# Second attention step with channels in the rows and eight transposes back to nodes, and a shorter reciprocal square root, in a four-layer graph network

## The chip, the core and the metric

The kernel runs on one core of one Trainium2 chip. The metric is the device time of one execution in microseconds; a kernel's number is the median of its runs. The engines are TensorE (PE; its weight loads are PEld), VectorE (DVE), ScalarE (ACT), GpSimd (POOL, which here issues the gathers) and SyncE (SP, which issues the other transfers). Each works through its own list of instructions in order, and they meet at semaphores.

## The reference

There are 8 graphs of 1024 nodes with 128 channels in float32, each with a 1024x1024 adjacency matrix of about 1.6% ones. Four layers follow each other, and each ends in `x = layernorm(x + layer(x))` without gain or bias:

```python
x = _layernorm(x + L0(adj, x))   # max over the first 25 neighbours of each node, then a projection and relu
x = _layernorm(x + L1(x, adj))   # graph attention with leaky relu scores, elu
x = _layernorm(x + L2(x, adj))   # the same with other weights
x = _layernorm(x + L3(x, adj))   # the layer that the change touches
```

The last layer is dot-product attention over the whole graph, applied twice:

```python
mask = where(adj == 1, 0.0, -1000.0)
score = (x @ att_W) @ x.T / sqrt(128)
att = softmax(score + mask, axis=-1)          # 1024 x 1024, the same in both steps
for W, b in ((W0, b0), (W1, b1)):
    y = tanh(att @ (y @ W + b))               # y starts as x
```

`_layernorm(x)` is `(x - mean) / sqrt(var + 1e-5)` over the 128 channels of a node.

## The kernel before

A graph's nodes are held as `xs[slot]`, eight tiles of 128 nodes in the partitions by 128 channels, for two graphs in turn (`slot`). Graphs 0 to 5 run in a hardware loop of three turns with two graphs each, graphs 6 and 7 are written out behind it. For each engine there is one function `graph(b, slot, in_loop)`, and its body is the order of that engine's work; nothing is planned by a program. Each also carries work for the graphs ahead, put by hand into places where the engine would wait:

- The neighbours' maximum of layer 0 for graph b+1 is made during graph b. POOL gathers 21 of the 25 neighbour rows of each tile of 128 nodes by indirect transfers, one instruction for each neighbour and tile (L483), 168 in a graph. The rows go into `gathered`, a ring of three tiles (`RING`). DVE reduces a tile with a maximum (`pool_tile`, L1132 and L1133), and `rows_pooled` frees the ring's place. So the gather of tile t waits for the pooling of tile t-3 (L476, L479), and for every pair of tiles also for the list of row numbers that DVE computes (`find_keys`, `find_members`, L1099, signal `rows_ready`). The table `SIDE` (L82) says in which place of DVE's order each of these pieces stands: tile 5 of graph b+1 stands at "last step", tile 6 at "half" and tile 7 at "end", all around the second attention step. POOL is one graph further ahead there: its gather of tile 0 of graph b+2 waits for the pooling of tile 6 of graph b+1.
- The other 4 neighbours of each node come from products with one-hot matrices: `make_hot` on ACT or DVE, `pick` on PE (16 matmuls of 512 columns each, L760) and `max_pick` on DVE (L1189), eight of them in a graph.
- `feed` converts and packs the adjacency of the graphs ahead (ACT L502, a transposing DMA, PE L707), and `count_first` with `take_count` counts neighbours (PE L735 to L740, ACT L526).

In the last layer PE makes the logits of a tile of 128 nodes (L942, L945), DVE its row maximum (L1315), ACT the exponential (L633); PE multiplies with a diagonal of reciprocals and so transposes it (L958), and ACT puts it into `probs_t` (L640), which holds the attention with source nodes in the partitions. The first step's product (`first_step`, L929) has the channels in the rows of its result: `values` (nodes by channels) is the stationary operand, 512 columns of `probs_t` the moving one. ACT takes tanh of each half of 512 nodes into `xt`, channels by nodes (L645), PE projects from it (L786), ACT copies the result to `values` (L571), and then comes the second step (L973 to L978):

```python
for t in range(T):
    for m in range(T):
        last = nc.tensor.matmul(low_t[:, t, :], probs_t[:, m, t * P:(t + 1) * P], values[:, m, 0:C], ...)
    if t % HALF == HALF - 1:
        att_heads.raised_by(last)
```

Here each matmul has a 128x128 block of the attention as stationary operand and 128 columns of `values` moving, so that the result has nodes in the rows. ACT takes tanh of each half (L655) into `head`, which is another view of `xt`'s memory, and DVE adds it to `xs` (L1334), makes the statistics of that half (`half_stats`, L1194), pools tile 6 between the two halves, and normalises (`layer_norm`, L1196). PE goes on with `feed`, `pick` 7 and the counting for graph b+2. In PE's trace a float32 matmul and its weight load stand as two records each, a transpose as one.

`layer_norm` is called four times in a graph. It aggregates the statistics, then computes the reciprocal square root for the 8 tiles on DVE with operations on 128x8 elements: add epsilon (L1203), shift right (L1204), subtract from a constant (L1206), three rounds of Newton's iteration of three operations each (L1209, L1210, L1212), and the offset for ACT (L1214). `link` puts a drain of DVE behind each. Then DVE scales the first four tiles (L1218) and ACT the other four (L563).

## Time and profile before

| | |
|---|---|
| median of 3 runs | 2911.93 us (2911.41 to 2938.62) |
| profiled execution, device time | 2927.49 us |
| its span in the trace | 2925.5 us |
| mean granted TensorE clock | 0.77 of full speed |
| PE busy | 1708.1 us (58% of the span) |
| PE weight loads | 1227.0 us (42%) |
| DVE busy | 1381.1 us (47%) |
| ACT busy | 923.4 us (32%) |
| POOL busy | 1258.4 us (43%), of it 1254.7 us in 1280 gather instructions (L483) |
| second attention step (L975) | 1024 matmul records, 118.7 us |
| first attention step (L929) | 256 matmul records, 131.3 us |
| tanh behind the second step (L655) | 16, 9.4 us |
| add behind it (L1334) | 16, 11.0 us |

The first three lines are times, the others come from the page of the profiled execution. No engine is busy for more than 58% of the span, so the busy times alone don't say what bounds the kernel. The profiled execution's time is 15.6 us above the median of the runs. A row of a timeline gives the start in us from the span's start, the busy time in us, the engine, the line of the kernel, the operation, its output and inputs, and how many instructions are merged in it; in brackets stands the idle time of the engine ahead of it and what ended it ("issue": nothing that the profile shows; "remote": a semaphore whose sender the profile can't name).

### The profile page before, as it was taken

The page shows a single profiled execution, that of the slowest core. Times are in us where ns is not written, and L with a number is a line of the kernel's source. Part 1 is how long each engine was busy: PE and PEld are TensorE (multiplying, and loading weights), DVE is VectorE, ACT ScalarE, POOL GpSimd, SP SyncE. Part 2 cuts the span into 40 slices and gives each one's busy share as a digit, 9 for nine tenths or more (in the row PEclk, how much of TensorE's full clock was granted, in tenths as well). Part 3 has the DMA queues.
Part 4 walks back from the last instruction along what each step waited for, and adds up shares of the span by engine and source line. Part 5 has one row for each costly group of instructions (what it writes and reads, how often), then busy time and mean ns, then how long its engine had stood idle before and what let it go on. Part 6 is the DMA issues. An engine that isn't in the chain of part 4 may idle for free.

```text
span 2925.5 us, 27567 instructions
## 1 busy us (share of the span) xinstructions
PE 1708.1 (58%) x8804; PEld 1227.0 (42%) x8804; DVE 1381.1 (47%) x3485; ACT 923.4 (32%) x1283; POOL 1258.4 (43%) x1307
## 2 busy tenths in 40 slices
PE   1655666536675367664475645646565555656778
PEld 0533553325443245342453434424353334534655
DVE  3654564336643347433464434544534445442642
ACT  1000433324333234333232343223422324223223
POOL 5366324553344553444444443544425544255000
PEclk9977677768787668876687866877778777787789
DMA  4221212222122221222222220222312222021001
GB/s 126 60 68 43 71 38 91 56 58 67 46 91 54 73 60 56 78 68 52 57 73 70 69 74 26 87 63 68 74 34 74 66 67 73 17 67 52 22 15 37
DMA packets 145466, 178.53 MB, mean 61 GB/s; under 512 B 91165, under 2 KB 108458, under 8 KB 145322
## 3 DMA queue, kind: packets, MB, share of 16 engines
q1 hardware_dynamic: 104362, 92.76, 11.5%
q0 software_dynamic: 40960, 83.97, 10.7%
q8 instruction: 76, 1.25, 0.2%
q14 instruction: 68, 0.56, 0.1%
HBM read 155.66 MB, written 4.19 MB: 55 GB/s over the span
## 4 chain that ended last, share of the span: by engine, by line
PE 36%; another core or an unknown queue 26%; issue 16%; DVE 11%; ACT 5%; DVEq 4%; DMA 1%; SPq 0%; ACTq 0%
PE big L860 5%; PE side L958 4%; PE spare L760 4%; PE big L929 3%; PE big L975 3%; PE big L786 3%; DVEq L68 3%; PE big L942 2%; PE big L807 1%; DVE pooled L1132 1%; PE big L760 1%; PE big L797 1%; PE big L851 1%; DVE stats L1194 1%
## 5 line engine op out<-in xcount | busy, mean ns | idle before, releaser
L483 POOL DMA_INDIRECT gathered<-in_x_dram,rows x1280 | 1254.7, 980 | 1445.0 <-DVE pooled L1133 648.4
L860 PE MATMUL big<-values,probs_t 128*128 128x129 f32 x1792 | 265.4, 303 | 147.6 <-issue 146.6
L760 PE MATMUL spare<-hot,x_part 128*128 128x512 f32 x1088 | 294.7, 420 | 52.1 <-issue 30.9
L860 PEld LDWEIGHTS big<-values,probs_t 128*128 128x128 f32 x1792 | 247.6, 216 | 166.2 <-issue 161.4
L760 PEld LDWEIGHTS spare<-hot,x_part 128*128 128x128 f32 x1088 | 213.1, 200 | 111.0 <-issue 64.6
L1132 DVE TENSOR_REDUCE pooled<-gathered 128x128 f32<-128x2688 f32 (+1 forms) x56 | 253.0, 4518 | 7.2 <-issue 6.9
L929 PE MATMUL big<-probs_t,values 128*128 128x512 f32 x256 | 131.3, 662 | 182.9 <-ACT probs_t L640 91.5
L958 PE MATMUL side<-recip_diag,work 128*128 128x128 f32 x1024 | 147.2, 294 | 114.2 <-issue 74.1
L1315 DVE TENSOR_REDUCE neg_max<-big 128x1 f32<-128x1024 f32 x64 | 78.3, 1224 | 277.7 <-remote 171.7
L958 PEld LDWEIGHTS side<-recip_diag,work 128*128 128x128 f32 x1024 | 134.4, 206 | 147.6 <-issue 129.3
L538 ACT ACTIVATE hot<-running,minus_count 128x2048 fp32r<-128x2048 bf16 x84 | 167.4, 1993 | 50.5 <-remote 41.2
L1249 DVE SCALAR_TENSOR_TENSOR probs_t<-row_gain,col_gain,adj_t 128x1024 f32<-128x1024 f32 x128 | 156.3, 1292 | 28.5 <-ACT row_gain L582 20.5
L541 ACT ACTIVATE hot<-hot,plus_one 128x2048 fp32r<-128x2048 f32 x84 | 168.2, 2003 | 2.7
L526 ACT CAST running<-spare 128x512 bf16<-128x512 f32 x92 | 53.9, 586 | 360.0 <-PE spare L740 152.2
L942 PE MATMUL big<-xt,row_gain 128*128 128x512 f32 x256 | 143.3, 686 | 38.4 <-issue 35.9
L1295 DVE TENSOR_TENSOR probs_t<-big,best_t 128x512 f32<-128x512 f32 x16 | 11.1, 692 | 309.8 <-PE big L900 270.5
L633 ACT ACTIVATE work<-big,neg_max 128x1024 f32<-128x1024 f32 x64 | 71.4, 1115 | 265.6 <-DVE neg_max L1315 180.0
L929 PEld LDWEIGHTS big<-probs_t,values 128*128 128x128 f32 x256 | 52.1, 214 | 244.8 <-issue 150.8
L797 PE MATMUL big<-ident,xs 128*128 128x128 f32 x256 | 57.6, 396 | 155.2 <-DVE xs L1218 119.6
L640 ACT COPY probs_t<-side 128x1024 f32<-128x1024 f32 x64 | 64.2, 1004 | 242.0 <-remote 178.3
L1189 DVE TENSOR_TENSOR best_t<-best_t,spare 128x512 f32<-128x512 f32 x52 | 35.8, 688 | 190.2 <-remote 123.4
L563 ACT ACTIVATE xs<-xs,offset,rstd 128x128 f32<-128x128 f32 x128 | 52.7, 482 | 222.9 <-DVE offset L1214 150.3
(182 smaller groups left out, 2689.4 us busy)
## 6 DMA issues: line engine op xcount, KB each, us to landing
adj_in<-in_adj_dram SPq DMA_DIRECT2D x128, 512.0 KB
gathered<-in_x_dram,rows POOLq DMA_INDIRECT x1280
xs<-in_x_dram SPq DMA_DIRECT2D x8, 512.0 KB
out_dram<-xs SPq DMA_DIRECT2D x8, 512.0 KB
adj_t<-adj_bf SPq DMA_TRANSPOSE x64
w_sb<-in_L_gnn_W_dram SPq DMA_DIRECT2D x1, 128.0 KB
w_sb<-in_L_gnn_W_dram SPq DMA_DIRECT2D x2, 64.0 KB
probs_t<-in_L_gnn_W_dram SPq DMA_DIRECT2D x1, 64.0 KB
```

What stands on the lines that cost most here:

```text
L68: self.settle()
L483: (late_gathered if late else rows_gathered[t % RING]).raised_by(pool.indirect_dma_start(out=gathered[:, t % RING, k * C:(k + 1) * C], out ...
L538: hot_apart.raised_by(nc.scalar.activation(hot[c][:, :, :], running[:, per * c:per * (c + 1), :], ACT.Abs, bias=minus_count[:, s:s + 1]))
L541: hot_made.raised_by(nc.scalar.activation(hot[c][:, :, :], hot[c][:, :, :].bitcast(F32), ACT.Relu, scale=-1.0, bias=plus_one[:, 0:1]))
L760: last = nc.tensor.matmul(pick_bank(b, q), x_parts[part][:, m, :], hot[c][:, m % per, :], start=(m == 0 and part == 0), stop=(m == T - 1 a ...
L786: last = nc.tensor.matmul(dst[:, t, :], xt[:, t * P:(t + 1) * P], w, start=not biased, stop=True, skip_group_check=True)
L860: last = nc.tensor.matmul(heads[:, t, 0:C + 1], probs_t[:, j, t * P:(t + 1) * P], values[:, j, :], start=False, stop=(j == T - 1), skip_gr ...
L929: last = nc.tensor.matmul(low[:, halves[h]], values[:, m, 0:C], probs_t[:, m, halves[h]], start=(m == 0), stop=(m == T - 1))
L942: nc.tensor.matmul((low, high)[t % 2][:, half], queries[:, t * P:(t + 1) * P], xt[:, half], start=True, stop=False, skip_group_check=True)
L958: last = nc.tensor.matmul(side_t[:, m, :], work[:, (t - 2) % 3, m * P:(m + 1) * P], recip_diag[:, t % 2, :], start=True, stop=True)
L1132: link(nc.vector.tensor_reduce(pooled[:, t, :], rows_of[:, :, 0:n], AX.X, ALU.max))
L1249: gat_probs.raised_by(nc.vector.scalar_tensor_tensor(out=probs_t[:, j, :], in0=row_gain[:, :], scalar=col_gain[:, j:j + 1], in1=adj_t[slot ...
```

## The change

The second attention step takes the first one's form: `first_step` is now `attend`, and both steps call it for the two halves of 512 nodes. ACT's tanh goes into `xt`, channels by nodes. The way back to nodes in the rows is new on PE: behind `feed`, and before `pick` 7, it waits for each half's tanh and transposes four 128x128 blocks of `xt` into the upper half of `big` (`high`). DVE's add waits for that (`head_turned`) and reads `high` in place of `head`. A new signal `head_added` tells PE before the next graph's layer 0 writes `high` that the adds are done, and ACT no longer waits for `x_normed` before it writes `xt` in layer 0.

In `layer_norm` the shift and the constant are one operation, and the three Newton rounds become one of three operations and a longer one of four.

```diff
+THIRD = 0.375 ** 0.5
-        head = xt[:, :].rearrange("p (t c) -> p t c", t=T)
-        guess = sb("guess", [P, T], I32)
+        head_turned = signal("head_turned", 2)
+        head_added = signal("head_added", 2)
...
             def take_xt(b, layer):
-                if layer == 0 and not (isinstance(b, int) and b == 0):
-                    act.wait_ge(x_normed.sem, x_normed.at(b, 0))
...
                 for h in range(2):
-                    tiles = slice(HALF * h, HALF * h + HALF)
                     act.wait_ge(att_heads.sem, att_heads.at(b, 2 + h + 1))
-                    att_tanh.raised_by(nc.scalar.activation(head[:, tiles, :], low_t[:, tiles, :], ACT.Tanh))
+                    att_tanh.raised_by(nc.scalar.activation(xt[:, halves[h]], low[:, halves[h]], ACT.Tanh))
...
                 project(low_t, w0_sb[:, 0, :], range(T), True)
+                if not (isinstance(b, int) and b == 0):
+                    pe.wait_ge(head_added.sem, head_added.at(b, 0))
...
                 pe.wait_ge(xw_ready.sem, xw_ready.at(b, 4))
-                for t in range(T):
-                    for m in range(T):
-                        last = nc.tensor.matmul(low_t[:, t, :], probs_t[:, m, t * P:(t + 1) * P], values[:, m, 0:C],
-                                                start=(m == 0), stop=(m == T - 1))
-                    if t % HALF == HALF - 1:
-                        att_heads.raised_by(last)
+                for h in range(2):
+                    att_heads.raised_by(attend(h, range(T)))
                 if exists(b, 1, B, in_loop):
                     feed(b, slot, 3, in_loop)
+                for h in range(2):
+                    pe.wait_ge(att_tanh.sem, att_tanh.at(b, 2 + h + 1))
+                    for t in range(HALF * h, HALF * h + HALF):
+                        last = nc.tensor.transpose(high[:, t * P:(t + 1) * P], xt[:, t * P:(t + 1) * P], ident[:, :])
+                    head_turned.raised_by(last)
+                if exists(b, 1, B, in_loop):
                     spare_maxed(b + 1, 6)
                     pick(b + 1, 7)
...
                 link(nc.vector.tensor_scalar(spread[:, :], moments[:, :, 1], EPS, None, ALU.add))
-                link(nc.vector.tensor_scalar(guess[:, :], spread[:, :].bitcast(I32), 1, None,
-                                             ALU.logical_shift_right))
-                link(nc.vector.tensor_scalar(rstd[:, :].bitcast(I32), guess[:, :], -1.0, RSQRT_GUESS,
+                link(nc.vector.tensor_scalar(rstd[:, :].bitcast(I32), spread[:, :].bitcast(I32), -0.5, RSQRT_GUESS,
                                              ALU.mult, ALU.add))
-                for _ in range(3):
-                    link(nc.vector.tensor_tensor(error[:, :], rstd[:, :], rstd[:, :], ALU.mult))
-                    link(nc.vector.scalar_tensor_tensor(out=error[:, :], in0=error[:, :], scalar=-0.5,
-                                                        in1=spread[:, :], op0=ALU.mult, op1=ALU.mult))
-                    link(nc.vector.scalar_tensor_tensor(out=rstd[:, :], in0=error[:, :], scalar=1.5,
-                                                        in1=rstd[:, :], op0=ALU.add, op1=ALU.mult))
+                link(nc.vector.tensor_tensor(error[:, :], rstd[:, :], rstd[:, :], ALU.mult))
+                link(nc.vector.scalar_tensor_tensor(out=error[:, :], in0=error[:, :], scalar=-0.5,
+                                                    in1=spread[:, :], op0=ALU.mult, op1=ALU.mult))
+                link(nc.vector.scalar_tensor_tensor(out=rstd[:, :], in0=error[:, :], scalar=1.5,
+                                                    in1=rstd[:, :], op0=ALU.add, op1=ALU.mult))
+
+                link(nc.vector.tensor_tensor(error[:, :], rstd[:, :], rstd[:, :], ALU.mult))
+                link(nc.vector.scalar_tensor_tensor(out=error[:, :], in0=error[:, :], scalar=-THIRD,
+                                                    in1=spread[:, :], op0=ALU.mult, op1=ALU.mult))
+                link(nc.vector.scalar_tensor_tensor(out=error[:, :], in0=error[:, :], scalar=THIRD * 10 / 3,
+                                                    in1=error[:, :], op0=ALU.add, op1=ALU.mult))
+                link(nc.vector.scalar_tensor_tensor(out=rstd[:, :], in0=error[:, :], scalar=1.875,
+                                                    in1=rstd[:, :], op0=ALU.add, op1=ALU.mult))
...
                 for h in range(2):
-                    dve.wait_ge(att_tanh.sem, att_tanh.at(b, 2 + h + 1))
-                    link(nc.vector.tensor_tensor(
-                        flat[:, halves[h]], flat[:, halves[h]],
-                        head[:, HALF * h:HALF * h + HALF, :].rearrange("p t c -> p (t c)"), ALU.add))
+                    dve.wait_ge(head_turned.sem, head_turned.at(b, h + 1))
+                    link(head_added.raised_by(nc.vector.tensor_tensor(
+                        flat[:, halves[h]], flat[:, halves[h]], high[:, halves[h]], ALU.add)))
                     half_stats(slot, h)
                     if h == 0:
                         side_work(b, slot, "half", in_loop)
```

## Rows read from the trace of the kernel before

**Rows 1.** The page, chain of work that ended last, by engine.

```profile
PE 36%; another core or an unknown queue 26%; issue 16%; DVE 11%; ACT 5%; DVEq 4%; DMA 1%; SPq 0%; ACTq 0%
```

**Rows 2.** Waits of POOL: who for whom, total us, times, longest us.

```profile
POOL gathered L483 <- DVE pooled L1133: 648.4, 23, 62.0
POOL gathered L483 <- DVE rows L1099: 417.4, 15, 30.7
```

**Rows 3.** Timeline of POOL, gathers that start behind a wait, graph 3 to 4.

```profile
1654.01 0.94 POOL L483 DMA_INDIRECT gathered<-in_x_dram,rows  x1 [28.77 <-DVE pooled L1133]
1736.12 0.94 POOL L483 DMA_INDIRECT gathered<-in_x_dram,rows  x1 [29.83 <-DVE rows L1099]
1772.85 0.94 POOL L483 DMA_INDIRECT gathered<-in_x_dram,rows  x1 [10.68 <-DVE pooled L1133]
1847.76 0.94 POOL L483 DMA_INDIRECT gathered<-in_x_dram,rows  x1 [48.95 <-DVE pooled L1133]
1928.76 0.95 POOL L483 DMA_INDIRECT gathered<-in_x_dram,rows  x1 [26.18 <-DVE rows L1099]
```

**Rows 4.** Timelines of DVE and of ACT while a gather of graph 3's attention runs.

```profile
1604.08 0.42 DVE L1051 MAX8 top_members<-keys 128x8 f32<-128x96 f32 x2 [4.36 <-issue]
...
1616.63 1.01 ACT L640 COPY probs_t<-side 128x1024 f32<-128x1024 f32 x1 [35.50 <-remote]
```

**Rows 5.** Busy time by engine (instructions), clock, DMA share, GB/s, inside gather.

```profile
1666.00:1706.50 40.50, 6.75 (x25) 3.00 (x23) 5.67 (x20) 3.03 (x6) 30.54 (x33) 0.57 0.24 66
```

**Rows 6.** Timelines of PE, ACT and DVE, second attention step of graph 3.

```profile
1635.94 14.56 PE L975 MATMUL big<-values,probs_t 128*128 128x128 f32 x128 [0.68 <-ACT values L571]
1650.34 0.56 PE L707 MATMUL packed<-pack_w,adj_t 128*128 128x32 bf16 x16
...
1643.83 2.00 ACT L541 ACTIVATE hot<-hot,plus_one 128x2048 fp32r<-128x2048 f32 x1
1645.73 0.58 ACT L655 ACTIVATE xt<-big 128x512 f32<-128x512 f32 x1
...
1646.35 0.69 DVE L1334 TENSOR_TENSOR xs<-xs,xt 128x512 f32<-128x512 f32 x1 [7.68 <-ACT xt L655]
1647.90 4.87 DVE L1132 TENSOR_REDUCE pooled<-gathered 128x128 f32<-128x2688 f32 x1
1652.85 0.35 DVE L1133 TENSOR_SCALAR pooled<-pooled,connected,pool_floor 128x128 f32<-128x128 f32 x1
```

**Rows 7.** Timeline of PE: eight records of the first step.

```profile
1583.14 3.60 PE L929 MATMUL big<-probs_t,values 128*128 128x512 f32 x8
```

**Rows 8.** Timeline of PE: four transposes of layer 0.

```profile
1717.55 0.60 PE L900 MATMUL big<-ident,pooled 128*128 128x128 f32 x4
```

**Rows 9.** Groups by line: count, busy us, mean ns, idle.

```profile
L1301 DVE SCALAR_TENSOR_TENSOR xs<-big,xs 128x512 f32<-128x512 f32 x16 | 10.8, 678 | 0.0
```

**Rows 10.** Timelines, graph 6's second step: PE, then DVE.

```profile
2715.15 16.84 PE L975 MATMUL big<-values,probs_t 128*128 128x128 f32 x128 [0.68 <-ACT values L571]
...
2725.59 0.69 DVE L1334 TENSOR_TENSOR xs<-xs,xt 128x512 f32<-128x512 f32 x1 [7.87 <-ACT xt L655]
```

**Rows 11.** Timeline of DVE, last graph's second add.

```profile
2914.92 0.69 DVE L1334 TENSOR_TENSOR xs<-xs,xt 128x512 f32<-128x512 f32 x1 [5.43 <-ACT xt L655]
```

**Rows 12.** Timeline of DVE, graph 6's last normalisation: first and last of 13 small operations.

```profile
2735.09 0.17 DVE L1203 TENSOR_SCALAR spread<-moments 128x8 f32<-128x8 f32 x1
...
2738.01 0.17 DVE L1214 SCALAR_TENSOR_TENSOR offset<-moments,rstd 128x8 f32<-128x8 f32 x1
```

**Rows 13.** Timeline of POOL: third to fifth tile's gathers behind graphs 1 and 5.

```profile
721.03 0.95 POOL L483 DMA_INDIRECT gathered<-in_x_dram,rows  x1 [16.97 <-DVE pooled L1133]
784.64 0.94 POOL L483 DMA_INDIRECT gathered<-in_x_dram,rows  x1 [37.42 <-DVE pooled L1133]
...
2122.17 0.95 POOL L483 DMA_INDIRECT gathered<-in_x_dram,rows  x1 [3.24 <-DVE pooled L1133]
2206.12 0.94 POOL L483 DMA_INDIRECT gathered<-in_x_dram,rows  x1 [57.99 <-DVE pooled L1133]
```

More of the change, by code:

```diff
@@ L923, in graph, with attend @@
                 pe.wait_ge(xw_ready.sem, xw_ready.at(b, 2))
-                def first_step(h, tiles):
+                def attend(h, tiles):
                     for m in tiles:
@@ L951, in graph @@
                     if t >= T:
-                        first_step(0, range(2 * (t - T), 2 * (t - T) + 2))
+                        attend(0, range(2 * (t - T), 2 * (t - T) + 2))
                     if t >= 2:
@@ L960, in graph @@
                         att_turned.raised_by(last)
-                att_heads.raised_by(first_step(0, range(4, T)))
+                att_heads.raised_by(attend(0, range(4, T)))
                 pe.wait_ge(att_t_ready.sem, att_t_ready.at(b, T))
-                att_heads.raised_by(first_step(1, range(T)))
+                att_heads.raised_by(attend(1, range(T)))
                 if exists(b, 1, B, in_loop):
```

## The prediction

> **What bounds the kernel now.** I read the chain of waits first. PE has 36% of it, and 42% goes to "issue" and to an unnamed releaser [rows 1]: time in which no engine is seen at work. A kernel bound by one engine would not look like this, so I asked what runs in that time. The waits of one engine answer: POOL, which only issues gathers, waits for DVE's pooling for 648 us and for DVE's row lists for 417 us [rows 2]. For the rest it gathers. Its timeline [rows 3] gives a graph's pattern: it starts at 1654.01, its next wait ends at 1736.12 and had begun 29.83 earlier, so two tiles (42 gathers) take 52.3 us, one tile 26.1. Eight tiles make 209 us of gathers in a period of 355.9 (from 1654.01 to 1928.76, plus 52.3 for the last two tiles and 28.8 for the wait that ends such a period).
>
> What the others do meanwhile is the second thing to see. In 40.5 us inside a gather PE issues 25 matmuls, DVE 20 and ACT 6 instructions, with nobody at work for most of it [rows 5]. Steps of a quarter of a microsecond take several there: 4.36 us idle ahead of a small maximum with no releaser but the drain before it, and an ACT copy comes 35.5 us late [rows 4]. The Trainium skill (Perfetto Trace Analysis, section on the tensor engine's instructions) says that a matmul's reported end is estimated, and its semaphore comes with PSUM's acknowledgement; this fits a copy that is released long after PE's recorded work, though the page does not tell why it would be 35 us. I don't need the cause. The engines run at full pace for some 12 us behind a gather's start, then crawl until a few us behind its end. So **the period is the gathers, of fixed length, and the stretches between them**, in which DVE's chain leads to the next start. The change must be costed stretch by stretch: what lengthens the chain to a gather's start counts in full, whatever PE is spared.
>
> **The second step and the transposes.** They stand in one such stretch, whose 28.77 us end when DVE has pooled tile 6 [rows 3, 6]. In it, before: PE begins the second step at 1635.94; its first half is ready 7.3 us later, but ACT is at work on a one-hot matrix until 1645.83, so tanh of the first half comes at 1645.73, DVE's add at 1646.35, its statistics, the pooling of tile 6 from 1647.90 to 1653.2, and the gather at 1654.01 [rows 6]. PE's second half, up to 1650.34, is off this path, behind the pooling.
>
> After: a record of 512 columns takes (3.60 - 0.59)/7 = 0.430 us [rows 7], where 0.59 is what the pipeline shows of a single one. The second step is 32 of them, 13.76 us to the next issue, where 128 records of 128 columns take 14.40 (1650.34 - 1635.94) [rows 6]. So a quarter of the records saves only 0.64 us a graph; the columns streamed are the same. But the first half's transposes stand behind both halves and behind the packing: 13.76, then 0.40 for the packing's issue (0.56 less its last record's tail), then four transposes of 0.60 together [rows 6, 8], end at 1650.70, and 0.05 for the signal: DVE's first add begins at 1650.75 and not at 1646.35. **This is +4.40 us on the path to the gather**, six times (graphs 0 to 5 are followed by such a gather): **+26.4**. The tanh is hidden in both cases: before, it waits for the one-hot matrix; after, it is done by 1646.4 while PE is still at the second half. The second half's tanh (0.60 behind PE's end) and transposes end by 1651.3, under the pooling of tile 6, and cost nothing while that pooling (5.2 us) covers them. What is queued behind PE's new waits is pick 7: it begins at 1651.3 instead of 1650.7 and needs 3.9 us, and DVE wants it only behind the normalisation, past 1660. The new wait on the adds in layer 0 concerns adds that a whole gather of two tiles lies behind, and ACT's removed wait came with one that PE's turned tiles satisfy later; both at nothing, within a microsecond either way, as an instruction more or less in a crawl.
>
> DVE's add now reads one operand from PSUM. The nearest row is the sum of layer 0, of the same size from PSUM, at 678 ns against 689 [rows 9, 6]: nothing. The Trainium skill (VectorE: DVE Perf Modes, the section on the TRN2 errata) gives 120 cycles as the fixed part from PSUM and 58 from SBUF, which speaks against the change: 62 cycles at 0.96 GHz on 16 adds are an estimated 1.0 us. By that the sum would be 1 us higher; the rows do not bear it out.
>
> Graph 6 has no gather behind it, yet its adds and the pooling between them are DVE's chain to the last graph. Its second step runs 16.84 us instead of 14.56, because the clock is at the lower level at first [rows 10], 2.28 more. There is no packing, so the first add comes at 2715.15 + 13.76 + 2.28 + 0.60 + 0.05 = 2731.84, not 2725.59 [rows 10]: **+6.2**. In the last graph nothing stands between the adds. Before, the second add begins 15.2 us behind the step's first record (14.56, the tanh's 0.60, signals) [rows 6, 11]. After, the transposes of the first half end at 14.4, its add and statistics hold DVE until 15.95, and the second add follows: **+0.8**.
>
> **The normalisation.** The shift and one operation of Newton's rounds less two: 12 operations ahead of the offset become 9. From the first to the offset it is 2738.01 - 2735.09 = 2.92 us, 0.243 each [rows 12], and the new ones are of the same kinds and size. Three less are 0.73 us, 32 calls, **-23.4**. Where do they lie? Layers 0 and 1 normalise in the stretches that end at the second and fourth start of [rows 3], on DVE's chain: certain, 16 calls, 11.7 us. So are three calls of graphs 6 and 7 that no gather covers. The other 13, of layers 2 and 3, stand in the first 12 us of a gather, whose length is fixed. There the gain is 0.73 us more of full pace before the crawl, and shows behind the gather as that much less to do, if the crawl begins with the gather's time. At the low end nothing of these 13 is saved (-13.9 in all), at the high end all, and more where one falls into a crawl. I take all, since each engine's work there hangs on the normalised tiles.
>
> **Sum**: 26.4 + 6.2 + 0.8 - 23.4 = **+10.0 us** (with the low end of the normalisation +19.5). On the profiled execution's 2927.5 that is 2937.5; it stands 15.6 us above the median of the runs, so the median becomes 2922. A measurement of this kernel can tell about 1% from no change, 29 us.
>
> **Rivals.**
> *The later gather is given back.* The engines have 4.4 us longer at full pace before it. For it: the crawl takes so much that any lead is worth a multiple. Against: all wait for DVE's normalisation, which stands behind the pooling and moves with it. If it were so, only the normalisation and PE's 0.64 would be left: 2911.9 - 23.4 - 8 x 0.64 + 7.0 (graphs 6 and 7), 2890.
>
> *The crawl falls otherwise, slower.* The two waits ahead of tiles 3 and 4 add up to 54.4 us behind graph 1, 59.6 in the period shown and 61.2 behind graph 5 [rows 3, 13]. What decides is how many records of pick 1 PE has through when the crawl takes hold behind the gather of tile 2, and a few tenths of a microsecond move it. Three of the six periods are of the cheap kind. If these go to 61.2, it is 3 x 6.8 = 20 us more: 2942, slower by 1.0%, and 2952 if layers 2 and 3 save nothing. The point from which it decides: pick 1's maximum on DVE comes later behind that gather's start than now. Against it: both the gather's start there and pick 1 hang on the same normalisation of layer 0 and should move together.
>
> *The crawl falls otherwise, faster.* The same spread the other way: three dear periods go to 54.4, -5.2 - 2 x 6.8 = -19: 2903. A normalisation that now runs into the crawl would add a few us. For 29 us less the first rival would have to come on top.
>
> *It doesn't do what it says*: if the weight loads or a clock at its lower level stretch the 512-column form, each half at 0.86 for a record would cost up to 13.8 us a graph, 110 in all. The first step, of the same form and operands, runs at 0.430 [rows 7], and PE is busy throughout here. I give it next to nothing.
>
> **How the numbers follow.** My forecast +10, within 10 us, has 0.50; the slower fall of the crawl 0.20, the faster 0.16, the lead given back 0.10, something else 0.04. The likeliest is 2922. The range reaches from the faster fall with some of the lead, 2898, to the slower fall, 2945, and leaves out about 2 in 10. Slower by over 1% (above 2941) is the upper part of the slower fall and half of the rest, 0.15; faster by over 1% (below 2883) needs two rivals at once, 0.06; the remainder is 0.79.
>
> **What would show it.** The second step's 32 records over 13.8 us and pick 7 behind 8 transposes; DVE's first add waiting for PE's transposes, 14.8 us behind the step's first record and not 10.4; the wait of POOL ahead of tile 0 near 33 us and not 29, six times; 9 small operations in 2.2 us in each normalisation; the waits ahead of tiles 2 and 6 shorter by 0.7. I am wrong if the first of these waits stays at 29, or if the sum of the waits ahead of tiles 3 and 4 moves by more than 3 us a graph.

## The result and the profile after

The changed kernel takes 2949.6 us (median of 20 runs, 2932.8 to 2964.9), the kernel before, beside it, 2926.2 (20 runs, 2911.4 to 2952.0). The ratio is **1.0058, interval 1.0035 to 1.0080**: about 17 us slower (10 to 23), under 1%, no change by the bound of the prediction. The two medians alone are 23.4 us apart, the upper end of that interval. A second comparison, with the last group of experiments, gave 1.0035 (1.0002 to 1.0069), +10 us. The forecast was +10, which is the lower end of the first interval. Its 2922 stood on the median of three runs, 2911.9; by 20 runs the kernel before is at 2926, so that 2949.6 lies 5 us above the end of the range, while 1.0058 times 2911.9, 2929, lies inside it.

PE has 704 records less; no other engine has more to do, and the chain is spread about as before [rows 1]. From the page, the span, the busy times and the chain:

```profile
span 2933.5 us, 25973 instructions
...
PE 1705.2 (58%) x8100; PEld 1173.6 (40%) x8100; DVE 1361.0 (46%) x3389; ACT 922.2 (31%) x1283; POOL 1255.9 (43%) x1307
...
PE 37%; another core or an unknown queue 25%; issue 18%; DVE 10%; ACT 4%; DVEq 3%; DMA 1%; SPq 1%; ACTq 0%
```

The second step of graph 3, PE, ACT and DVE in order of time:

```profile
1657.51 14.00 PE L929 MATMUL big<-probs_t,values 128*128 128x512 f32 x32 [0.68 <-ACT values L570]
...
1667.30 0.58 ACT L653 ACTIVATE xt<-big 128x512 f32<-128x512 f32 x1
...
1671.35 0.55 PE L705 MATMUL packed<-pack_w,adj_t 128*128 128x32 bf16 x16
...
1671.55 0.60 ACT L653 ACTIVATE xt<-big 128x512 f32<-128x512 f32 x1 [3.67 <-PE big L929]
...
1671.75 1.10 PE L979 MATMUL big<-ident,xt 128*128 128x128 f32 x8
1672.43 0.69 DVE L1341 TENSOR_TENSOR xs<-xs,big 128x512 f32<-128x512 f32 x1 [14.47 <-PE big L979]
...
1672.61 3.91 PE L758 MATMUL spare<-hot,x_part 128*128 128x512 f32 x16
...
1674.00 4.78 DVE L1133 TENSOR_REDUCE pooled<-gathered 128x128 f32<-128x2688 f32 x1
1678.85 0.34 DVE L1134 TENSOR_SCALAR pooled<-pooled,connected,pool_floor 128x128 f32<-128x128 f32 x1
...
1681.55 0.17 DVE L1204 TENSOR_SCALAR spread<-moments 128x8 f32<-128x8 f32 x1
...
1684.04 0.17 DVE L1221 SCALAR_TENSOR_TENSOR offset<-moments,rstd 128x8 f32<-128x8 f32 x1
```

Compare this with [rows 6]. PE has 32 records over 13.84 us to the next issue (1671.35 - 1657.51) instead of 128 over 14.40. The first half's tanh is done at 1667.88 and nobody uses it for four microseconds, because PE is at the second half. Then come the eight transposes, and DVE's add begins 14.92 us behind the step's first record, where it stood at 10.41. What follows is as before: 7.59 us from the add to the gather (before 7.66). The normalisation takes 2.49 us from its first small operation to the offset here (one of them took 0.40) and 2.18 to 2.64 in all 32 calls; before, the calls at full pace took 2.91 to 3.30, the one of [rows 12] 2.92. POOL's timeline has the same five starts as [rows 3]:

```profile
1680.02 0.94 POOL L484 DMA_INDIRECT gathered<-in_x_dram,rows  x1 [35.46 <-DVE pooled L1134]
...
1761.14 0.94 POOL L484 DMA_INDIRECT gathered<-in_x_dram,rows  x1 [28.89 <-DVE rows L1100]
...
1791.31 0.94 POOL L484 DMA_INDIRECT gathered<-in_x_dram,rows  x1 [4.15 <-DVE pooled L1134]
...
1867.30 0.94 POOL L484 DMA_INDIRECT gathered<-in_x_dram,rows  x1 [50.08 <-DVE pooled L1134]
...
1950.90 0.94 POOL L484 DMA_INDIRECT gathered<-in_x_dram,rows  x1 [28.42 <-DVE rows L1100]
```

Ahead of tile 0, POOL waits 35.5 instead of 28.8 us, and 31.5 us more over the six graphs; ahead of tiles 3 and 4 it waits 22.5 less over seven graphs. But a total from one execution says little. I split the wait ahead of tile 0 at two instructions, the step's first record and DVE's first add. Each number is in us and a mean over six graphs; the profiles other than the first two were taken with the experiments below:

```
profiled execution               wait   gather's end   first record   add to
                                        to record      to add         start
before                           29.5   11.4           10.40          7.66
changed                          34.8   12.3           14.92          7.59
changed, second profile          39.8   17.3           14.92          7.59
old normalisation, new step      36.4   13.9           14.92          7.59
new normalisation, old step      33.4   15.3           10.40          7.66
the same, second profile         32.5   14.4           10.40          7.66
```

The columns on the right do not vary by 0.1 us among the six graphs of an execution. **The middle one is the change: +4.52, less 0.07 behind it, +4.45 us a graph; the forecast had +4.40.** The left one is what the crawl of the gather before leaves over, 10.7 to 20.0 us in single graphs. The two profiles of the changed kernel differ by 5.0 a graph in it. That is 30 us of a span, three times the effect sought. They come from two groups of runs, in which the kernel before stood at 2926 and at 2967 us, so part of these 30 us may belong to the group and not to the single execution; the two profiles of the normalisation alone, with the kernel before at 2963 and 2967, differ by 0.9. Within one execution of this table the graphs differ by up to 7.4 us.

### The profile page after: what moved, and what is told of

The parts are those of the page before. It is cut to its first block, busy times and chain, and to the rows that moved or that the text cites. A ratio compares the mean times of both kernels' runs of the same rounds, so it can differ in the third digit from the quotient of the medians.

```text
span 2933.5 us, 25973 instructions
## 1 busy us (share of the span) xinstructions
PE 1705.2 (58%) x8100; PEld 1173.6 (40%) x8100; DVE 1361.0 (46%) x3389; ACT 922.2 (31%) x1283; POOL 1255.9 (43%) x1307
## 3 DMA queue, kind: packets, MB, share of 16 engines
q0 software_dynamic: 40960, 83.97, 10.7%
## 4 chain that ended last, share of the span: by engine, by line
PE 37%; another core or an unknown queue 25%; issue 18%; DVE 10%; ACT 4%; DVEq 3%; DMA 1%; SPq 1%; ACTq 0%
PE big L929 7%; PE spare L758 6%; PE big L858 6%; PE side L958 4%; DVEq L69 2%; PE big L942 2%; PE big L784 2%; DMA adj_t<-adj_bf 1%; DVE probs_t L1256 1%; PE big L805 1%; DVE pooled L1133 1%; PE big L849 1%; PE big L758 1%; ACT adj_less L512 1%
## 5 line engine op out<-in xcount | busy, mean ns | idle before, releaser
L929 PE MATMUL big<-probs_t,values 128*128 128x512 f32 x512 | 245.1, 632 | 188.1 <-issue 126.7
L758 PE MATMUL spare<-hot,x_part 128*128 128x512 f32 x1088 | 314.7, 442 | 55.9 <-issue 45.8
L758 PEld LDWEIGHTS spare<-hot,x_part 128*128 128x128 f32 x1088 | 228.5, 215 | 116.9 <-issue 67.9
L929 PEld LDWEIGHTS big<-probs_t,values 128*128 128x128 f32 x512 | 101.0, 204 | 310.4 <-issue 244.5
L539 ACT ACTIVATE hot<-running,minus_count 128x2048 fp32r<-128x2048 bf16 x84 | 167.6, 1995 | 23.4 <-remote 22.1
L604 ACT ACTIVATE work<-work 128x512 f32<-128x512 f32 x32 | 20.0, 626 | 333.6 <-DVE work L1267 307.2
```

The source lines that it names most:

```text
L539: hot_apart.raised_by(nc.scalar.activation(hot[c][:, :, :], running[:, per * c:per * (c + 1), :], ACT.Abs, bias=minus_count[:, s:s + 1]))
L758: last = nc.tensor.matmul(pick_bank(b, q), x_parts[part][:, m, :], hot[c][:, m % per, :], start=(m == 0 and part == 0), stop=(m == T - 1 a ...
L929: last = nc.tensor.matmul(low[:, halves[h]], values[:, m, 0:C], probs_t[:, m, halves[h]], start=(m == 0), stop=(m == T - 1))
```

## The experiments

Ratios are to the kernel before, timed on the same chip in five rounds. The first four ran together (before 2963.1 us, 23 runs).

**1. The normalisation alone** (new lines of the normalisation, all else as before).

> The kernel before with the change's shorter normalisation alone. My theory: 3 operations of 0.243 us less in 32 calls, all on the path, so 23 us less than before: ratio 0.992; the wait ahead of the gather of tile 2 (30.4 us on average in the trace of before) 0.7 us shorter, each normalisation 2.19 us instead of 2.92 from its first small operation to the offset. Rival A, that the 13 calls under a gather save nothing: 14 us less, 0.995. Rival B, that a lead won ahead of a crawl is worth a multiple: 40 us less or more, 0.986.

Measured 0.9945 (0.9918 to 0.9972), and in a second comparison, with the last group below, 0.9922 (0.9896 to 0.9949): 16 and 23 us less. The 23.4 of the forecast is in both intervals (8 to 24, 15 to 31). Its low end, 13.9, by which a normalisation under a gather saves nothing, is in the first and a microsecond outside the second, so the two lean against that view without settling it. The 40 us of rival B are outside both. The wait ahead of tile 2 is 29.7 and 28.8 us a graph, against 30.4 before: shorter, as expected, by 0.7 and 1.6.

**2. The second step alone** (the change, with the normalisation of before).

> The change without its shorter normalisation: second step in the first one's form, eight transposes, adds from PSUM. My theory: the first add stands 14.9 us behind the step's first record instead of 10.4, the gather of tile 0 starts that much later in six graphs and graph 6 and 7 lose 7 us together: 33 us more than before, ratio 1.011 (POOL's wait ahead of tile 0 near 34 us instead of 29.5). Rival, that the later gather is given back because the engines have longer at full pace: 2 us more, 1.001, with the waits ahead of the later tiles shorter by 4.4 us a graph in sum.

Measured 1.0107 (1.0052 to 1.0161), +32 us (15 to 48), against 33.4 by the sum and 2 by the rival that a later gather is given back. The rival is out. With the two measurements of the normalisation, -16 and -23, the parts add up to +15 and +9, as the whole does (+17 and +10).

**3. The first half turned early.** The first half's four transposes go between the fourth and the fifth block of the second half. `turn_head(h)` is the change's wait and its four transposes for one half; the second half's stay behind `feed`:

```diff
-                for h in range(2):
-                    att_heads.raised_by(attend(h, range(T)))
+                att_heads.raised_by(attend(0, range(T)))
...
+                attend(1, range(4))
+                turn_head(0)
+                att_heads.raised_by(attend(1, range(4, T)))
```

> The change with one thing moved: PE makes the first half's four transposes in the middle of the second half's 32-record product (behind 4 of its 8 blocks) and not behind all of it and the packing. The tanh of the first half is ready 10.4 us behind the step's first record, PE reaches the transposes at 10.4. My theory: first add at 11.1 us behind the first record instead of 14.9, POOL's wait ahead of tile 0 near 31 us instead of 34.8, 3.8 us less in seven graphs: 26 us less than the change, ratio to before 0.997. Rival, that the start of this gather is not what counts: as the change, 1.006.

Measured 0.9974 (0.9940 to 1.0007), where 0.997 was expected. PE and DVE in graph 3:

```profile
1650.20 10.57 PE L929 MATMUL big<-probs_t,values 128*128 128x512 f32 x24 [0.68 <-ACT values L570]
...
1660.62 0.65 PE L977 MATMUL big<-ident,xt 128*128 128x128 f32 x4
...
1661.31 0.69 DVE L1346 TENSOR_TENSOR xs<-xs,big 128x512 f32<-128x512 f32 x1 [8.43 <-PE big L977]
```

The first add comes 11.11 to 11.13 us behind the step's first record in every graph with a gather, not 14.92, which leaves 0.71 over the 10.40 of before, some 4 us in six graphs. Against the normalisation alone in the same group (0.9945) the step as such now costs 0.0029, some 9 us, and not the 32 of experiment 2. So the place of the transposes made up 3.81 of the 4.52 us a graph; the 0.71 that stay are near the 0.60 of four transposes [rows 8]. The number of transposes was not varied. POOL's wait ahead of tile 0 is 33.4 in this profile and not the 31 expected: the part ahead of the first record is 14.6 here.

**4. Pooling moved behind both adds, in the kernel before.** PE does nothing else there; only DVE's chain to the gather gets longer.

```diff
-                    if h == 0:
-                        side_work(b, slot, "half", in_loop)
+                side_work(b, slot, "half", in_loop)
```

> The kernel before with one thing moved: DVE pools tile 6 behind both adds of the second attention step and not between them. No work is added, only the start of the gather of tile 0 comes later: the second add can begin at 15.2 us behind the step's first record, its statistics end at 16.8, the pooling at 22, so the gather starts 4.8 us later, and the normalisation 5 us later too. My theory: 29 us more than before in six graphs and 5 in graph 6, ratio 1.012, with a wait ahead of tile 0 near 34.3 us. Rival, that a later gather is given back: 1.000 to 1.003.

Measured 1.0109 (1.0052 to 1.0166), +32 us (15 to 49). DVE and POOL in graph 3:

```profile
1690.28 0.69 DVE L1334 TENSOR_TENSOR xs<-xs,xt 128x512 f32<-128x512 f32 x1 [7.69 <-ACT xt L655]
...
1696.65 4.75 DVE L1132 TENSOR_REDUCE pooled<-gathered 128x128 f32<-128x2688 f32 x1
...
1702.64 0.94 POOL L483 DMA_INDIRECT gathered<-in_x_dram,rows  x1 [40.68 <-DVE pooled L1133]
```

From the add to the gather it is 12.36 us instead of 7.66, 4.70 a graph. Six times that is 28, and 33 with the 5 us expected of graph 6. So a delay of this chain costs about its own length, though no part of the change is in it. This is the premise of the prediction; the interval is 17 us to either side, enough to put out the rival (0 to 9 us) but not to fix the price of a microsecond. The normalisation is delayed too in this run, so it does not tell the gather's start from the work behind it. The wait ahead of tile 0 came out as 38.6 us and not the 34.3 expected, again by its left part (15.8).

**5 to 8. A group without the crawl.** The next group was meant to test the rest on the same ground. It met other conditions: the kernel before took **1914.95 us** there (9 runs, 1912.4 to 1920.1).

> The kernel before with the new normalisation (measured alone at 0.9945 of before), and on ACT the tanh of the second step's first half put between the two halves of the one-hot matrix of pick 7, instead of behind both. Nothing is left out. In the timeline of before the first half's product is there 7.3 us behind the step's first record, and ACT reaches the tanh only at 9.8, because 8 us of one-hot work stand ahead of it; between the halves it can begin at 7.3. My theory (what shortens DVE's chain to a gather's start counts in full, six times): the first add, the pooling of tile 6 and the gather come 2.45 us earlier, 6 x 2.45 = 14.7 us or 0.0050, ratio to before 0.9895, wait ahead of tile 0 shorter by 2.5; pick 7's one-hot is ready at 13.3 behind the first record, ahead of PE's end of the step at 14.4, and costs nothing. Rival (a lead ahead of a gather is lost behind it, because the work behind the pooling then runs into the crawl): 0.9945, the wait ahead of tile 0 shorter by 2.5 but that ahead of tile 2 longer by as much.

> The kernel before with the new normalisation (0.9945 of before), whose two rounds of Newton's method (7 operations of 0.243 us, 1.70 us) are left out in the 16 calls of layers 2 and 3, so that these use the first guess of the reciprocal root. 13 of these calls stand in the first 12 us of a gather, 3 (graphs 6 and 7) do not. My theory (a shorter chain there is more full pace ahead of the crawl and shows behind the gather): 16 x 1.70 = 27.2 us, ratio to before 0.9945 - 0.0092 = 0.985, the waits ahead of tiles 2 and 6 shorter by 1.7 each against the run with the new normalisation. Rival (under a gather nothing is saved): 3 x 1.70 = 5.1 us, 0.993. A third view, that a lead ahead of the crawl is worth a multiple, would give less than 0.980.

> The same seven operations left out in the 16 calls of layers 0 and 1 instead, which stand between gathers, on DVE's chain to the next gather's start. This is the yardstick for the run on layers 2 and 3. My theory: 16 x 1.70 = 27.2 us, ratio to before 0.985, as there. The rival that a normalisation under a gather saves nothing says the same of this run, 0.985, but 0.993 of the other. If the sum of the waits ahead of tiles 3 and 4 reacts to when pick 1 stands to the crawl, this run moves that and the other does not: then the ratio lies outside 0.982 to 0.988.

> The changed kernel with DVE's pooling of tile 6 ahead of both adds of layer 3 instead of between them, so that this gather no longer waits for the transposes. Nothing is left out. DVE idles long enough ahead of the first add to hold the pooling (5.2 us), so the gather of tile 0 starts some 14 us earlier, and the wait ahead of tile 0 falls from 35 to about 20 us, six times. The normalisation of layer 3 and all that hangs on it then begin some 9 us behind the gather's start and not 1, and lose 8 us of full pace ahead of the crawl. My theory (full pace between the gathers counts, not the start alone): the wait ahead of tile 2 grows by 8 to 12 us, a net gain of 2 to 6 us a graph, 12 to 36 us in all, ratio to before 0.994 to 1.002. Rival (the gather's start alone counts, and the normalisation of layer 3 is covered by the gather): 6 x 14 = 84 us less than the changed kernel, ratio to before 0.977, the wait ahead of tile 2 as it was.

The edits: in the first, on ACT, behind the lines of the new normalisation,

```diff
-                    make_hot(b + 1, 7)
+                    make_hot(b + 1, 7, range(1))
...
                 for h in range(2):
+                    if h == 1 and exists(b, 1, B, in_loop):
+                        make_hot(b + 1, 7, range(1, CHUNKS))
```

in the second and third `if rounds:` ahead of the seven operations, with `rounds` false in the layers named (these two leave out work that the result needs, to measure its price), and in the fourth

```diff
+                side_work(b, slot, "half", in_loop)
                 for h in range(2):
...
-                    if h == 0:
-                        side_work(b, slot, "half", in_loop)
```

Measured, in this order: 0.9876 (0.9858 to 0.9894), 0.9836 (0.9816 to 0.9856), 0.9857 (0.9839 to 0.9874), 0.9850 (0.9835 to 0.9866). The second and third lie where my theory had them (0.985 for both), the first and fourth outside of it (0.9895, and 0.994 to 1.002). Neither confirms or refutes anything: all four expectations were made for a kernel in which POOL waits. POOL's waits in the first of these runs are

```profile
POOL gathered L484 <- issue: 384.2, 1260, 0.6
POOL gathered L484 <- DVE rows L1102: 26.8, 7, 20.2
POOL gathered L484 <- DVE pooled L1136: 26.6, 13, 8.4
```

That is 53 us for DVE against 1,066 [rows 2]. What is gone can be seen in windows of 40.5 us inside the gathers (busy us and instructions of PE, PE's weight loads, DVE, ACT and POOL; clock, DMA share, GB/s). The first is of this run, the other of the second profile of the changed kernel, where the engines crawl, and begins 11 us behind a gather's start:

```profile
1480.00:1520.50 40.50, 27.01 (x184) 20.06 (x184) 25.70 (x61) 23.48 (x29) 30.75 (x33) 0.83 0.48 137
```

```profile
1712.00:1752.50 40.50, 7.06 (x26) 3.11 (x25) 5.98 (x21) 3.13 (x7) 30.44 (x34) 0.58 0.24 68
```

POOL issues as many gathers (33 and 34) in the same time; PE executes 184 instructions and not 26. The two windows do not hold the same stretch of a graph, but where this run is at the same distance behind the second step's first record as the other window, PE executes 151. The engines' own durations are alike: a pooling takes 4803 ns in the median there and 4.87 us in [rows 6]; the second step's 14.56 us are the same, and the first add stands 8.15 to 8.16 us behind its first record in all eight graphs. In this group a graph takes 215 to 220 us, of which some 210 are gathers (168, one every 1.25 us): the start of a gather is hardly ever waited for. The two runs with seven operations less, in the layers under gathers and in those between, are equal within their intervals, and say nothing on where the crawl gives a microsecond back; that stays open. With the new normalisation's 23.4 and their own 27.2 us, they save 31 and 27 of 50.6 us, 0.62 and 0.54 of it. The change itself was not timed there.

**9 to 12. With the crawl again.** The last group repeats four kernels as they stand. It met the crawl again (before 2966.7 us, 23 runs).

> The changed kernel itself, unedited, because the last group of runs showed the kernel before at 1914.95 us and not at some 2940: a chip on which the engines do not crawl during gathers and POOL waits 53 us in all for DVE and not over 1,000. What is asked is whether the change has the same worth there. If this group meets a chip with the crawl (before near 2940): 1.006, as in the first comparison. If it meets one without (before near 1915): my theory is that the price of the transposes was paid in POOL's waits ahead of tile 0 and that without such waits the gathers cover most of it, while the shorter normalisation stays on the chain of each graph: 0.993 of before. Rival (the change costs the same microseconds on any chip): +10 to +17 us, 1.005 to 1.009.

> The kernel before with the new normalisation alone, unedited. On a chip with the crawl: 0.9945 as measured. On one without: leaving out 27.2 us more of the normalisation in layers 2 and 3 gave 0.9836, in layers 0 and 1 0.9857. If a microsecond of it counts in full there, these would be 50.6 us or 0.9736; they are 0.62 and 0.54 of that, so that I expect 0.6 x 23.4 = 14 us: 0.9927. Rival (in full): 23.4 / 1915, 0.988.

> The kernel with the new normalisation and the tanh between the halves of the one-hot matrix, unedited, for the comparison with the run of the normalisation alone on the same chip. On a chip with the crawl: mine 0.9895 (0.0050 under the normalisation alone), rival 0.9945 (a lead ahead of the gather is lost behind it). On one without: 0.9876 as measured, of which the tanh's part is what the normalisation alone leaves; with 0.9927 for that, 0.0051.

> The changed kernel with tile 6's pooling ahead of both adds, unedited, beside the changed kernel on the same chip. On a chip with the crawl: mine 0.994 to 1.002 with the wait ahead of tile 0 at about 20 us and that ahead of tile 2 grown by 8 to 12; rival 0.977 with the wait ahead of tile 2 as it was. On one without: 0.985 as measured, which is 0.008 under what I expect of the changed kernel.

The changed kernel gave 1.0035 and the normalisation 0.9922, as told above. **The tanh between the halves** gave 0.9899 (0.9855 to 0.9943), where 0.9895 was expected. Beside the normalisation of its own group, though, it is 0.0023 less and not 0.0050, and the interval can tell it neither from that nor from nothing. Its timelines, of ACT, DVE and POOL in graph 3:

```profile
1646.69 0.60 ACT L658 ACTIVATE xt<-big 128x512 f32<-128x512 f32 x1 [1.57 <-PE big L978]
1647.18 2.00 ACT L539 ACTIVATE hot<-running,minus_count 128x2048 fp32r<-128x2048 bf16 x1
1647.32 0.69 DVE L1343 TENSOR_TENSOR xs<-xs,xt 128x512 f32<-128x512 f32 x1 [5.44 <-ACT xt L658]
...
1654.96 0.94 POOL L484 DMA_INDIRECT gathered<-in_x_dram,rows  x1 [29.34 <-DVE pooled L1136]
```

ACT waits 1.57 us for PE, as it should; the add comes 8.16 us behind the first record (1639.16), not 10.40. That is 2.24 us a graph and 13.5 in six (forecast 14.7). POOL's waits ahead of tile 0 fall by 18.3 in six graphs against the profile of the normalisation alone in this group, of which 4.8 lie ahead of the first record and are not the edit's; those ahead of tile 2 rise by 5.0. So what the lead is worth in the end stays open.

**The pooling ahead of both adds**: 0.9879 (0.9838 to 0.9921), 44 us under the changed kernel (2976.5 to 2932.4). I had 12 to 36 (0.994 to 1.002 of before), the rival 84 (0.977): both missed. DVE and POOL in graph 3:

```profile
1664.76 4.85 DVE L1133 TENSOR_REDUCE pooled<-gathered 128x128 f32<-128x2688 f32 x1
1669.69 0.35 DVE L1134 TENSOR_SCALAR pooled<-pooled,connected,pool_floor 128x128 f32<-128x128 f32 x1
1680.85 0.69 DVE L1342 TENSOR_TENSOR xs<-xs,big 128x512 f32<-128x512 f32 x1 [10.81 <-remote]
...
1687.53 0.17 DVE L1204 TENSOR_SCALAR spread<-moments 128x8 f32<-128x8 f32 x1
...
1691.46 0.17 DVE L1215 SCALAR_TENSOR_TENSOR error<-error,spread 128x8 f32<-128x8 f32 x1 [0.53 <-issue]
1692.86 0.17 DVE L1217 SCALAR_TENSOR_TENSOR error<-error 128x8 f32<-128x8 f32 x1 [1.23 <-issue]
...
1695.66 0.17 DVE L1221 SCALAR_TENSOR_TENSOR offset<-moments,rstd 128x8 f32<-128x8 f32 x1 [1.23 <-issue]
```

```profile
1670.85 0.94 POOL L484 DMA_INDIRECT gathered<-in_x_dram,rows  x1 [29.38 <-DVE pooled L1134]
...
1707.21 0.94 POOL L484 DMA_INDIRECT gathered<-in_x_dram,rows  x1 [10.45 <-DVE pooled L1134]
...
1758.38 0.94 POOL L484 DMA_INDIRECT gathered<-in_x_dram,rows  x1 [25.25 <-DVE rows L1100]
```

The gather starts 14.0 us earlier, as reckoned (the six waits fall by 83.7 in all, against the second profile of the changed kernel). The work that followed it at full pace now meets the crawl. The first add, 10 us behind the gather's start, already comes 18.70 us behind the step's first record (1662.15) instead of 14.92. The normalisation stands 17 us behind the gather's start: 8.13 us to the offset instead of 2.49, with 1.23 idle ahead of an operation of 0.17. The pooling of tile 7 stands behind it, and so a wait is there that no other profile has: POOL stops between tiles 0 and 1, 10.45 us, 62.7 in six graphs. The wait ahead of tile 2 is shorter, by 25.2 in six, and not longer. These three make 46.2 us of waits less, but those ahead of tiles 3 and 4 are 10.9 longer and those ahead of tile 6 9.0. All of POOL's waits together fall by 30.8, and the two profiled executions differ by 34.2; the medians' 44 is not explained to the microsecond. The mechanism was right (full pace behind the start is lost) and its place wrong: I had it ahead of tile 2.

This kernel and the one with the tanh between the halves are under the kernel before in both kinds of group, and under the changed kernel where that was timed. Together the two edits were not tried.

## Why the prediction was right, point by point

- **What bounds the kernel.** Shown, where there is the crawl: experiment 4 lengthens one chain by 4.7 us six times and costs 32 (15 to 49). In the group without it POOL hardly waits, and the premise does not hold. Experiment 12 adds a limit: a start 14 us earlier gave back 44 of 84 us, so the start of the gather is not all that counts.
- **+4.40 us to the first add**, on which the sum rests: measured +4.52, with -0.07 behind it. The term came from a record's spacing, the packing's issue and four transposes, all of them rows of before, and the experiments on the step alone and on the early transposes bear it out. Six times 4.45 is 26.7 (forecast 26.4).
- **Graph 6**, forecast +6.2: the add moves from 10.44 to 16.96 us behind the step's first record, +6.5 (17.00 in the second profile). **The last graph**, second add: from 15.23 to 16.04, +0.8 as forecast.
- **One operand from PSUM** at nothing: the 16 adds take 0.67 to 0.69 us, as before. The Trainium skill (VectorE: DVE Perf Modes, the section on the TRN2 errata) gives a longer fixed part from PSUM, an estimated 1.0 us in all; the trace does not agree: the median of the 16 is 684 ns with one operand from PSUM and was 692 with both from SBUF.
- **The normalisation**, forecast -23.4: most calls are 0.7 to 1.1 us shorter, as said or a little more. What reaches the end is 16 and 23 us by two measurements. The prediction called the 16 calls of layers 0 and 1 certain to lie between gathers at full pace. That is not always so: a call of layer 1 took 4.61 and one 4.91 us in the kernel before, and three took 5.04 to 8.50 in the second profile of the changed kernel. Whether the calls under a gather count in full stays open.
- **Pick 7 behind the transposes, the waits of ACT and PE**: pick 7 begins 15.10 us behind the step's first record instead of 14.80, and DVE takes its result at 1685.39 with 0.16 us idle ahead (before 0.17). The trace names nobody who waits for the adds.
- **The rivals.** "Given back" is out by experiment 2. "The crawl falls otherwise, faster" is what the first profile of the changed kernel shows, waits ahead of tiles 3 and 4 of 384 us in seven graphs and not 406. But the other profiles with the crawl have 381 to 406, with no order by what was changed, and the second profile of the changed kernel has 393. I take it for a draw of each execution or group, not an effect of the change. "The crawl falls otherwise, slower" would be more than 406, and no profile shows it. So my sign of error, "more than 3 us a graph", was met in the first profile (3.2) and not in the second (1.8), and meant nothing: the bound was inside the spread between executions, which I had taken from the graphs of one.
- **The waits ahead of tiles 2 and 6**, forecast 0.7 shorter each: ahead of tile 2 it is 1.6 and 1.1 less a graph in the two profiles, ahead of tile 6 it is 0.8 and 1.7 more. The second sign failed, and why the wait ahead of tile 6 grew is not shown; it is 190 to 209 us over seven graphs in every other profile with the crawl, and 188 in the one of before.
- **The wait ahead of tile 0 "near 33"** came out as 34.8 and 39.8: my 4.4 is in it, and the left column of the table too.
- **The level.** The median of three runs was 14 us below that of twenty. The forecast of the difference was off by 7 us in the first comparison and by nothing in the second, where the measurement itself is good to 7 to 10 us; that of the absolute time was off by 28. That +10 was met this closely is in part luck: it is the difference of +33.4 and -23.4, and each of these is measured only to some 8 to 16 us.

## What to carry to other kernels

Split a wait at instructions whose distance doesn't vary from one repetition to the next, and price the edit on that part; a total over one profiled execution can differ by three times the effect. A half that is finished early should be consumed where it is finished: moving four transposes from behind the second half into its middle gave back 3.8 of 4.5 us a graph. And where the engines crawl inside gathers, the work placed just behind a gather's start has a stretch of full pace, which is lost to it when the gather starts ahead of that work (a normalisation of 2.49 us took 8.13).

## What the runs showed of the hardware

The kernel before ran in 1915 us in one group of comparisons and in 2926 to 2967 us in the others. In the first the mean granted TensorE clock of the profiled executions is 0.90 to 0.91 and not 0.76 to 0.77, but PE's busy time falls only from 1708 to 1541 us, which is little of the 1000 us between the kernel's times. Most of the rest is idle time inside gathers. In the other groups, and not in this one, the engines that do not gather advance in steps from some 10 to 13 us behind a gather's start: 1.23 us idle ahead of a DVE operation of 0.17, and 26 PE instructions in 40.5 us. POOL issues its gathers 1.25 us apart in both. The gathers' packets also take the same time on the DMA engines, 10.7% of 2925.5 us (kernel before) and 16.6% of 1902.1 us (the first run of that group), 313 and 316 us. What differs between the groups no run here shows. The record numbers the chip 11 for the first four experiments and 0 for both later groups, the one without the crawl and the one with it, so the chip's number does not tell them apart. For a reader it means that a ratio found under one condition need not hold under the other, and that the kernel before should be timed beside each comparison.
